# Third attention of a four-block network: the order of the transposed score matmuls of two head pairs

## The reference

```python
qkv = (x @ qkv_w).reshape(b, n, 3, H, D)          # b=16, n=256, H=16, D=16
scores = jnp.einsum('bhnd,bhmd->bhnm', q, k) * D ** (-0.5)
scores = jnp.where(node_mask[:, None, None, :], scores, -jnp.inf)
attn = jax.nn.softmax(scores, axis=-1)
out = jnp.einsum('bhnm,bhmd->bhnd', attn, v).transpose(0, 2, 1, 3).reshape(b, n, c)
attn_out = out @ proj_w + proj_b
x = x + gate_msa * _modulate(_layernorm(attn_out), shift_msa, scale_msa)
```

## Time and profile before

| | us |
|---|---|
| time, median of 3 runs | 3444.59 |
| lowest and highest run | 3440.4, 3445.57 |
| profiled execution, span from first to last instruction | 3442.1 |
| third attention in it (from 1461 to 1943) | 482 |
| one entry in the middle of it (from 1703.26 to 1732.04) | 28.8 |

### The profile page before, as it was taken

One profiled execution on the slowest core, in us unless ns is written; L12 is line 12 of the kernel. 1 busy time (PEld: TensorE's weight loads), 2 busy tenths in 40 slices (PEclk: granted clock), 3 DMA queues, 4 the chain that ended last, 5 costly groups with the idle time before them and its releaser, 6 DMA issues. The chain is left out here.

```text
span 3442.1 us, 71017 instructions
## 1 busy us (share of the span) xinstructions
PE 3093.8 (90%) x26346; PEld 2530.8 (74%) x26346; DVE 2204.7 (64%) x4255; ACT 1694.4 (49%) x3085; POOL 804.7 (23%) x656
## 2 busy tenths in 40 slices
PE   7899999998898969999999699789999999994697
PEld 5777877776798969877777598567777776772686
DVE  4566656665666766667777567657575757567674
ACT  3344444443454435545555445556666666662364
POOL 1221122111112321112222211322122222221453
PEclk8999999999899989999999899899999999997798
DMA  5000000000110010010000100100000000004243
GB/s 159 10 6 6 3 6 6 6 3 7 43 24 20 0 47 0 6 44 0 0 0 0 57 19 18 29 7 0 0 0 0 0 0 0 0 1 125 84 128 71
DMA packets 64656, 80.66 MB, mean 23 GB/s; under 512 B 9666, under 2 KB 56514, under 8 KB 64308
## 3 DMA queue, kind: packets, MB, share of 16 engines
q1 hardware_dynamic: 58436, 71.13, 6.9%
q0 software_dynamic: 6144, 8.52, 1.3%
HBM read 66.80 MB, written 12.85 MB: 23 GB/s over the span
## 5 line engine op out<-in xcount | busy, mean ns | idle before, releaser
L915 POOL TENSOR_TENSOR L0a_prob<-L0a_prob 128x1024 f32<-128x1024 f32 x48 | 117.3, 2444 | 571.9 <-PE L0a_o L1270 571.9
L1017 ACT ACTIVATE L0a_prob<-L0a_st 128x512 f32<-128x512 f32 x256 | 138.7, 597 | 201.5 <-PE L0a_st L1237 174.8
L921 POOL TENSOR_TENSOR L3a_shift<-L3a_neg,L3a_mx 128x256 fp32r<-128x256 f32 x128 | 95.7, 747 | 554.4 <-DVE L3a_mx L1496 552.4
L1017 ACT ACTIVATE L3a_prob<-L3a_st 128x512 f32<-128x512 f32 x256 | 138.8, 597 | 128.5 <-PE L3a_st L1237 128.5
L1496 DVE TENSOR_REDUCE L0a_mx<-L0a_s 128x2 f32<-128x512 f32 x256 | 164.4, 684 | 39.2 <-PE L0a_s L1213 37.4
L1845 ACT ACTIVATE L2a_prob<-L2a_st 128x512 f32<-128x512 f32 x256 | 132.2, 604 | 116.1 <-PE L2a_st L1876 116.1
L1486 DVE SCALAR_TENSOR_TENSOR L3a_qk_lo<-raw,cols_sb,L3a_qk_hi 128x256 fp32r<-128x256 f32 x256 | 156.5, 651 | 36.5 <-ACT L3a_qk_hi L1008 36.5
L1496 DVE TENSOR_REDUCE L3a_mx<-L3a_s 128x2 f32<-128x512 f32 x256 | 163.8, 680 | 18.1 <-PE L3a_s L1213 18.1
L2108 DVE TENSOR_REDUCE L2a_mx<-L2a_s 128x2 fp32r<-128x512 f32 x256 | 163.5, 681 | 15.2 <-PE L2a_s L1876 15.2
L1435 DVE RECIPROCAL L0a_rsum<-L0a_sum 128x256 f32<-128x256 f32 x16 | 28.1, 1758 | 197.8 <-PE L0a_sum L1285 176.2
L1435 DVE RECIPROCAL L3a_rsum<-L3a_sum 128x256 f32<-128x256 f32 x16 | 28.1, 1758 | 174.4 <-PE L3a_sum L1285 155.4
(11 more groups left out here) (615 smaller groups left out, 11488.6 us busy)
## 6 DMA issues: line engine op xcount, KB each, us to landing
raw<-in_moe_w SPq DMA_DIRECT2D x16, 1024.0 KB, 8.6
x_sb<-in_x SPq DMA_DIRECT2D x1, 4096.0 KB, 25.1
L0a_gate<-gate_rows SPq DMA_DIRECT2D x32, 128.0 KB, 3.9
L0m_gate<-gate_rows SPq DMA_DIRECT2D x32, 128.0 KB, 3.8
L2a_gates<-gate_rows SPq DMA_DIRECT2D x2, 2048.0 KB, 9.5
L2m_gate<-gate_rows SPq DMA_DIRECT2D x32, 128.0 KB, 3.8
out_x<-x_sb SPq DMA_DIRECT2D x1, 4096.0 KB, 17.6
token_rows<-x_sb SPq DMA_DIRECT2D x1, 4096.0 KB, 29.4
```

The costliest lines, as they stand in the source:

```text
L915: nc.gpsimd.tensor_tensor(both[:, :, :, 0:N], both[:, :, :, 0:N], both[:, :, :, N:2 * N], ALU.add).then_inc(halves_done, 1)
L921: nc.gpsimd.tensor_tensor(shift[:, u % 4, :, :, :], neg64[:].unsqueeze(1).unsqueeze(1).to_broadcast([P, 2, TT, 64]), mx[:, u % 2, :, :].un ...
L1017: A(prob[:, u % 4, h, :], st_ps[u % 2][h][:], ACT.Exp, scale=64 ** -0.5).then_inc(p_done, 1)
```

## The change

`scores_t` now takes the step's two pairs together. The loop over the pair stands inside that over the terms, so that each term goes to the four row groups in turn. Since pair A and pair B are no longer apart, the two waits that stood between them stand ahead of both.

```diff
             def body(i, first, final):
-                def scores_t(w):
+                def scores_t(u):
+
                     for kt in range(TT):
                         ks = slice(N + kt * P, N + (kt + 1) * P)
                         for n, (a, b) in enumerate(((qk_hi, qk_hi), (qk_lo, qk_hi), (qk_hi, qk_lo))):
-                            for h in range(2):
-                                last = mm(st_ps[w % 2][h][:, kt * N:(kt + 1) * N], a[rows(w, h), w // 2, ks], b[rows(w, h), w // 2, 0:N],
-                                          start=(kt == 0 and n == 0), stop=(n == 2))
-                                if kt == TT - 1 and n == 2:
-                                    last.then_inc(st_done, 1)
+                            for w in range(2):
+                                for h in range(2):
+                                    last = mm(st_ps[w][h][:, kt * N:(kt + 1) * N], a[rows(w, h), u, ks], b[rows(w, h), u, 0:N],
+                                              start=(kt == 0 and n == 0), stop=(n == 2))
+                                    if kt == TT - 1 and n == 2:
+                                        last.then_inc(st_done, 1)
...
-                    scores_t(2 * u)
                     if u == 1 and not final:
                         pe.wait_ge(xlo_done, i + 2)
                     if u == 3 and not first:
                         pe.wait_ge(taken, i)
-                    scores_t(2 * u + 1)
+                    scores_t(u)
```

## The result

The changed kernel is slower: 3468.61 us median (3461.73 to 3470.72) against 3445.08 for the kernel before on the same chip, ratio 1.0068, interval 1.0054 to 1.0082 (the 3444.59 of the prediction is the median of the three runs of before that were there then). That is 23.5 us where 5.7 were forecast, outside the range.

The account below looks back on a forecast made before the run. The prediction took TensorE, busy for 90% of the span, as the bound. The moved wait's 7.35 us less the gain of 1.65 made +5.7 us, a median of 3450.3 from 3444.59; range 3445 to 3455.

Parts of the forecast that it names:

- The block: In every step's block: six slots of four weight loads at pitch 0.116 us instead of nine slots, ending 0.35 us earlier.
- The rival with slower slots: In every block, four row groups at once run slower; 0.01 us a slot costs 3.8 us, giving 3454.1; chance 0.08.
- The gain: Step 0, at the wait of `values`: 0.11 us saved in each of 15 entries, 1.6 us in all; other steps 0.
- The rival by which all steps gain: The block's 0.35 us is won in all 64 steps, 22.4 us less the moved wait's 7.35, giving 3429.5; chance 0.07.
- the one by which the row groups' own queues undo the new order: In the blocks, the interleaving is undone and only the moved waits count: 3451.9; taken as the forecast's upper side.
- The moved wait of step 1: Step 1's block waits for VectorE's split of the next entry's tokens and starts 0.49 us later: 15 x 0.49 = 7.35 us.
- The rival by which this wait costs nothing: Some link of step 1 has unseen slack, so only -1.65 us is left: 3442.9, no change; chance 0.07.
- The fear that the change of the array's form would begin only behind the wait: Ahead of step 1's block, the array's drain starts after the wait: up to 0.90 us each, 13.5 in all; not adopted.
- The moved wait of step 3: Step 3's block, behind VectorE's taking of the projection, starts up to 0.04 us later; price 0, or 0.6 us if passed on.
- The step that failed: From step 1's late block down the chain to step 2's: no link has slack, so the whole 0.49 us arrives, price 7.35.
- the 0.28 that the prediction gave to "slower": Whole kernel: total chance of slower by over 0.2%, of it 0.21 from the main forecast and 0.07 from four groups running slower.
- A sign that was too tight: Stages outside the third attention: the prediction is wrong if any of them changes by more than a microsecond.

Follow-up runs that it names:

- e2: Changed kernel with the interleaved block in steps 0 and 2 alone, steps 1 and 3 in the old order with the wait between the pairs: 3440.08 us, ratio 0.9997.
- e5: Changed kernel with step 1 alone put back to the old order, its wait between the pairs: 3439.50 us, ratio 0.9983.
- e1: Changed kernel with the old order of the block (pair A, then pair B) in all steps, both waits still ahead of pair A: 3466.28 us, ratio 1.0079.
- e6: Changed kernel with the block interleaved in step 1 alone, its wait ahead; steps 0, 2 and 3 in the old order: 3467.66 us, ratio 1.0064.
- e3: Changed kernel plus seven matmuls with unused result in step 1, between `scores` and the wait of `over`: 3447.82 us, ratio 1.0009.
- e7: Changed kernel plus three matmuls with unused result in step 1's idle time ahead of `over`: 3457.60 us, ratio 1.0040.
- e4: Changed kernel with the next entry's `transposes` and their wait moved ahead of `scores` in step 0: 3444.57 us, ratio 1.0010.
- e10: The same kernel as e5, run again on another chip with more rounds: 3440.16 us, ratio 0.9996.
- e8: Changed kernel with the two moved waits as the first of the step's waits instead of the last: 3467.47 us (one run).
- e9: e5 with step 1's wait of `over` split, its first half waiting for the second exponential only: 3433.84 us, ratio 0.9975.

## Why the prediction was wrong, point by point

- **The block**: right. Six slots with four loads each, at a pitch of 0.12, in all steps. Entry 8, step 1, the second to the last slot:

```profile
1718.96 0.22 PEld L1876 LDWEIGHTS L2a_st<-L2a_qk_hi,L2a_qk_lo 32*128 32x128 f32 x4
1719.08 0.23 PEld L1876 LDWEIGHTS L2a_st<-L2a_qk_lo,L2a_qk_hi 32*128 32x128 f32 x4
1719.20 0.22 PEld L1876 LDWEIGHTS L2a_st<-L2a_qk_hi 32*128 32x128 f32 x4
1719.32 0.22 PEld L1876 LDWEIGHTS L2a_st<-L2a_qk_hi,L2a_qk_lo 32*128 32x128 f32 x4
1719.44 0.22 PEld L1876 LDWEIGHTS L2a_st<-L2a_qk_lo,L2a_qk_hi 32*128 32x128 f32 x4
...
1719.87 0.60 ACT L1845 ACTIVATE L2a_prob<-L2a_st 128x512 f32<-128x512 f32 x1 [1.85 <-PE L2a_st L1876]
```

  The first exponential comes 1719.87 - 1718.86 = 1.01 behind the block's start, as before. The rival with slower slots is out.
- **The gain**: right, 0.11 in step 0, nothing elsewhere. `values` now waits for the second exponential (0.36 of idle time), and its load at 1712.83 stands 2.14 behind the block instead of 2.25. e2 and e5 show the gain by itself. The rival by which all steps gain is out: the waits for exponentials took it, 63 instead of 32. So is the one by which the row groups' own queues undo the new order: its rows above show four loads in each slot.
- **The moved wait of step 1**: right in kind, 0.05 to 0.06 short in size. Step 0 grew by 0.43 instead of 0.38; the rest is the sequencer's semaphore instruction, of which no row of before had told me (I had taken the 0.05 that a single wait shows). Over 14 entries that is 0.8 us. The rival by which this wait costs nothing is out. The fear that the change of the array's form would begin only behind the wait was unfounded: the whole distance from the split's end to the first load is 0.115. The 0.41 of the earlier trace rows was idle time of the weight loads alone; in the matmul rows of before above, the block's matmuls start at 1710.99 while those of `weighted` run to 1711.05.
- **The moved wait of step 3**: right in its price, nothing, short in its size. Step 2 is 0.11 longer, where up to 0.04 was forecast, and step 3 0.10 shorter. The forecast's list was off in itself there: it lets both grow, to 8.18 and 5.5, and its four steps add up to 29.19 where its sum has 29.16.
- **The step that failed** is the one that follows the moved wait down the chain: "Each link follows the one before without slack, so the whole 0.49 reaches step 2", price 7.35. In it the added idle time costs what it lasts. I had read that the clock stands at its upper level over this stage and took that as a given of the stage; but it depends on what TensorE does, and the change more than doubled TensorE's idle time at one place in each entry. The term that is missing is ten falls at 1.50 us, 15.0 of the 17.6 us in the profiled execution, and more than that in the other three, if their mean clock says what it seems to. e1 and e6 show that the moved wait brings the falls, e3 that they go when the idle time is filled again and the kernel is otherwise the same, e7 that with less of it filled they come back. Of the 0.28 that the prediction gave to "slower", nothing stood for this cause; that the time came out on that side is no merit of it.
- **A sign that was too tight**: I had called myself wrong if other stages changed by more than a microsecond. They did, by 3.3, with nothing changed in them; single executions scatter by more than that sign allowed.

The Trainium skill, "TensorE: Matmul & The Clock Gate", Part 1, What's actually happening, says that the clock follows how busy TensorE has been recently. The trace agrees, and the runs put a price to it here, 1.50 us a fall. The same page of the Trainium skill, section HAM oscillation, describes falls by long waits for transfers between matmuls; in the changed kernel none of the three idle times was over 1.00 us.

**Why in one entry and not in another.** The amount of idle time alone doesn't decide: e4 had more of it than e7 and fewer falls, and e10 had one with the idle time of before. The traces on record show that the entry's place in time decides with it. In the changed kernel the falls begin 30.72 us apart (1691.5, 1722.2, 1752.9), and they do so in e1, e6, e7 and e8 as well wherever they come in a row, though the entries themselves last from 30.67 to 31.11 us there. So the clock changes on a beat of its own, an even grid of times that runs on while the entries drift past it. In each of the twelve traces all changes of the clock in this stage lie on one such grid. The table places the 168 loop entries of the twelve traces on it, by the start of step 1's block:

| idle time in step 1 | block starts less than 1 us behind a beat | of them with a fall | other entries | of them with a fall |
|---|---|---|---|---|
| 0.68 or less (before, e2, e3, e5, e9, e10) | 19 | 1 | 65 | 0 |
| 1.07 and 1.19 (e7, e4) | 12 | 8 | 16 | 0 |
| 1.50 to 1.82 (after, e1, e6, e8) | 37 | 37 | 19 | 7 |

The seven falls of the last field stand within 1.2 us of a beat. At the same place in time, then, the idle time decides between a fall in each entry and nearly none, which is the cause shown once more; away from that place no idle time of these kernels brought a fall. It also tells why falls come in rows: an entry with a fall lasts 30.7 us in the changed kernel, the distance of the falls, so the next block starts at the same place of the beat, while an entry without one lasts 29.2 and moves on. In e7 an entry with a fall lasts 30.7 too, and the six stand in a row. In e4 it lasts 30.1, so a second one didn't follow. How many falls a kernel has therefore hangs on the length of its entries and on where its first block meets the beat, and 10, 11 and 12 say little of a ranking. In e3 only two entries started at such a place; that its zero is no luck rests on the 17 others of the first row, one of which had a fall.

**What stays open.** How much idle time in that place is enough: between 0.68 and 1.50 us the same place brought a fall in some entries and none in others. Nor did I see a trace of the changed kernel's longer runs.

## What to carry to other kernels

Where TensorE is the bound and its clock is at the upper level, an idle time on it can cost more than it lasts: before moving a wait ahead of work that now covers it, add up TensorE's idle times near the place before and after, and put a price on a fall from the rows (here the work that follows took 1.5 us more). Read the number of falls over many entries, since it hangs on where the entries happen to lie. A block of work that gets shorter in front of a wait for another engine gives nothing but more idle time; split or move that wait first, as e9 did. Whether the clock is the cause can be tested cheaply, by filling the idle time with matmuls that nobody reads.

## What the runs showed of the hardware

- The granted clock of TensorE was 0.50 from 1722.20 to 1725.60, after 1.63 us of idle time in three pieces of 0.50, 0.13 and 1.00, and so in ten of 14 entries, at 1.50 us each. Over all twelve traces, with 1.50 us of idle time or more each of the 37 blocks that started less than 1 us behind a beat of the clock's changes had such a fall, with 0.68 or less one of 19.
- Seven added matmuls of 128x256 per entry took the ten falls away: a median of 3447.82 (ratio 1.0009) where the same kernel without them has 3468.61 (1.0068).
- Four row groups loaded and multiplied at once at the pitch of two, 0.12 us a slot, with 256 columns.
- A wait among several at one matmul took 0.115 us from VectorE's end to the first load where it was the late one at the list's end, 0.304 at its head, against 0.054 for a single one.
